# A mixture-of-experts layer on one core: the short chunk's down products stacked, shorter routing, four weight chunks split later

## The chip, the cores and the metric

The kernel runs on one core of a Trainium2 chip. The metric is the device time of one execution in microseconds (us), as a median over runs. A tile here has 128 partitions; T is 512 tokens.

## The reference, cut to what matters

Inputs: x of 8 groups x 1024 tokens x 256, float32. The first layer adds a gated linear scan (`q * scan(sigmoid(a), kv)` of three projections of a normalised x). The second layer adds a mixture of experts:

```python
logits = jnp.einsum('GSM,ME->GSE', x, router_w)          # 8 experts
dispatch, combine = _gating_top2(logits, C)              # C = 256 places per group and expert
expert_inputs = jnp.einsum('GSEC,GSM->EGCM', dispatch, x)
layer_w0 = jnp.einsum('EGCM,EMH->EGCH', expert_inputs, w0_kernel)   # H = 1368
layer_w1 = jnp.einsum('EGCM,EMH->EGCH', expert_inputs, w1_kernel)
hidden = jax.nn.gelu(layer_w0, approximate=True) * layer_w1
expert_outputs = jnp.einsum('EGCH,EHM->EGCM', hidden, wo_kernel)
out = jnp.einsum('EGCM,GSEC->GSM', expert_outputs, combine)
```

A token goes to its two best experts; a place number of 256 or more drops it. Every product is made in float32r with operands split into a high part (rounded) and a low part (the rest): high x high + high x low + low x high. The router's product is made in float32.

## The kernel before, in words

All order is written out by hand, engine by engine, with semaphores between them; nothing is a loop on the chip.

**Phase 1** has a step per group g (`step`). TensorE projects the group (`third`, line 1503: 12 blocks of 6 products with 512 columns), transposes (1519, 1532, 1544), and for the group before makes the router's logits (`route`, 1556: the 128 tokens of a tile are the stationary operand, the router's 8 columns stream; 4 tiles x 2 halves, each float32 product being two passes, so 16 loads and products per half group), and the running count of masks (`count`, 1563 and 1567). VectorE chooses the two experts of the group two back (`choose`, 16 instructions) and places its tokens (`place`, 12 instructions), between scans, residuals and statistics. ScalarE makes sigmoids, normalisations, the router's input `x2nT` (799) and the exponent (803). GpSimd scatters records (gates, token, source) to their slots (658) and gathers rows (677). Between these, ScalarE (813, 814) and VectorE (1211, 1223) split expert 0's weight chunks as they arrive: `first_chunks` says which chunks in which step.

**Phase 2** has 8 experts x 4 tiles of 512 rows. The hidden size 1368 goes in 11 chunks: 10 of 128, and the short chunk, number 8, with 88 = 64 + 24. Per chunk TensorE makes gate (1691) and value (1714; 1705 for the short chunk), 6 products of 512 columns each, and two chunks later the down products of chunk hc - 2, in four blocks j of 128 rows: high x (high | low) with 512 columns (1730) and low x high with 256 (1732). At the tile's end the down products of chunks 8, 9 and 10 stand in a row. The chain of a chunk: gelu on ScalarE (912; 906, 907 and a copy 910 for the short one), product on VectorE (1440; 1429, 1434, 1437 for the short one), high part on ScalarE (922), low part on VectorE (1443), down products. ScalarE's and VectorE's programs keep this order, so gelu of chunk hc + 1 stands behind the high part of chunk hc. In the fourth tile `next_weights(e, hc - 3)` follows on both engines from chunk 3 on (895, 896; 1211, 1418), and for the last three chunks in the next expert's first tile. Row blocks are scaled by the gates (956, 1410) and added to the output by GpSimd (726).

**The drain.** The first two tiles of expert 0 run beside the last groups' remaining steps (`drain(t, hc)`); there the down products use three products of 256 columns each (1725, 1727, 1732), as in the last tile of all. The last tile keeps the down products of chunks 5 to 10 to its end (`down_rows`). TensorE waits for all 11 of expert 0's splits before it begins tile 0.

## Time and profile before

| | us |
|---|---|
| median of 3 runs | 1645.25 |
| lowest, highest | 1642.83, 1646.39 |
| the profiled execution's own time | 1658.51 |
| its span | 1656.8 |
| TensorE, VectorE, ScalarE, GpSimd busy | 1620.5, 939.8, 762.3, 506.1 |

A row of a timeline has the start, the duration, the engine (PE TensorE products, PEld its weight loads, DVE VectorE, ACT ScalarE, POOL GpSimd), the line, the operation, the tiles written<-read, and in brackets how long the engine was idle before it and for whom. "x2" means that two like instructions are merged. The mean granted TensorE clock was 0.993 of full.

### The profile page before, as it was taken

The page shows a single profiled execution, that of the slowest core. Times are in us where ns is not written, and L with a number is a line of the kernel's source. Part 1 is how long each engine was busy: PE and PEld are TensorE (multiplying, and loading weights), DVE is VectorE, ACT ScalarE, POOL GpSimd, SP SyncE. Part 2 cuts the span into 40 slices and gives each one's busy share as a digit, 9 for nine tenths or more (in the row PEclk, how much of TensorE's full clock was granted, in tenths as well). Part 3 has the DMA queues.
Part 4 walks back from the last instruction along what each step waited for, and adds up shares of the span by engine and source line. Part 5 has one row for each costly group of instructions (what it writes and reads, how often), then busy time and mean ns, then how long its engine had stood idle before and what let it go on. Part 6 is the DMA issues. An engine that isn't in the chain of part 4 may idle for free.

```text
span 1656.8 us, 22948 instructions
## 1 busy us (share of the span) xinstructions
PE 1620.5 (98%) x8450; PEld 1396.0 (84%) x8450; DVE 939.8 (57%) x1955; ACT 762.3 (46%) x1389; POOL 506.1 (31%) x433
## 2 busy tenths in 40 slices
PE   7999899799999999999999999999999999999998
PEld 6888788688888888888888888888888888888887
DVE  7999754345644564447544654466445644475453
ACT  5777545234433453336333543345334533453333
POOL 2156566563222222222222222222222222222211
PEclk9999999899999999999999999999999999999999
DMA  7553121025422342225211522243223422351211
GB/s 169 160 160 122 53 80 45 13 41 120 86 38 37 81 93 37 39 43 124 39 36 36 135 38 39 39 109 71 39 39 82 93 36 38 64 109 33 36 13 13
DMA packets 193848, 110.94 MB, mean 67 GB/s; under 512 B 96008, under 2 KB 189640, under 8 KB 193736
## 3 DMA queue, kind: packets, MB, share of 16 engines
q1 hardware_dynamic: 165064, 75.37, 18.1%
q0 software_dynamic: 28672, 34.10, 12.8%
q8 instruction: 67, 1.10, 0.3%
q14 instruction: 45, 0.37, 0.1%
HBM read 60.11 MB, written 34.61 MB: 57 GB/s over the span
## 4 chain that ended last, share of the span: by engine, by line
PE 79%; DVE 6%; issue 4%; ACT 3%; SPq 3%; POOL 2%; DMA 2%; another core or an unknown queue 1%; POOLq 0%; ACTq 0%; DVEq 0%
PE bank L1691 23%; PE bank L1714 21%; PE bank L1730 14%; PE bank L1732 8%; PE bank L1503 7%; DVE y L1440 2%; PE bank L1556 1%; PE bank L1705 1%; SPq L509 1%; ACT hhi L922 1%; DVE hlo L1443 1%; SPq L426 1%; POOL slots L658 1%; POOL out L726 1%
## 5 line engine op out<-in xcount | busy, mean ns | idle before, releaser
L726 POOL DMA_INDIRECT out<-xring,slot_records x128 | 215.4, 1683 | 858.1 <-DVE xring L1410 792.9
L922 ACT ACTIVATE hhi<-y 128x512 fp32r<-128x512 f32 (+1 forms) x349 | 220.8, 633 | 508.7 <-DVE y L1440 427.6
L1730 PE MATMUL bank<-wo,hhi 128*128 128x512 f32 (+1 forms) x1276 | 443.7, 385 | 2.0 <-DVE hlo L1443 1.8
L1440 DVE TENSOR_TENSOR y<-bank,sig 128x512 f32<-128x512 f32 x320 | 220.9, 690 | 334.1 <-PE bank L1714 300.8
L1732 PE MATMUL bank<-wo,hlo 128*128 128x256 f32 x1396 | 382.2, 274 | 0.1
L1443 DVE TENSOR_TENSOR hlo<-y,hhi 128x512 fp32r<-128x512 f32 (+1 forms) x349 | 241.6, 692 | 243.9 <-ACT hhi L922 237.6
L912 ACT ACTIVATE sig<-bank 128x512 f32<-128x512 f32 x320 | 189.6, 593 | 209.2 <-PE bank L1691 181.9
L1730 PEld LDWEIGHTS bank<-wo,hhi 128*128 128x128 f32 (+1 forms) x1276 | 239.1, 187 | 50.5 <-DVE hlo L1443 4.0
L1732 PEld LDWEIGHTS bank<-wo,hlo 128*128 128x128 f32 x1396 | 261.6, 187 | 9.2 <-issue 0.8
L1691 PE MATMUL bank<-xThi,whi 128*128 128x512 f32 (+1 forms) x704 | 217.0, 389 | 7.4 <-issue 3.5
L1691 PE MATMUL bank<-xTlo,whi 128*128 128x512 f32 (+1 forms) x704 | 213.2, 383 | 0.0
L1691 PE MATMUL bank<-xThi,wlo 128*128 128x512 f32 (+1 forms) x704 | 212.7, 383 | 0.0
L1714 PE MATMUL bank<-xThi,whi 128*128 128x512 f32 x640 | 192.9, 381 | 1.2 <-DVE y L1440 0.8
L1714 PE MATMUL bank<-xTlo,whi 128*128 128x512 f32 x640 | 192.2, 380 | 0.0
L1714 PE MATMUL bank<-xThi,wlo 128*128 128x512 f32 x640 | 192.2, 380 | 0.0
L677 POOL DMA_INDIRECT rows<-x_rows,slot_records x128 | 129.4, 1011 | 122.0 <-DMA out<-xring,slot_records 88.6
L1691 PEld LDWEIGHTS bank<-xTlo,whi 128*128 128x128 f32 (+1 forms) x704 | 132.3, 188 | 27.0
L658 POOL DMA_INDIRECT slots<-records,sloti x128 | 128.3, 1002 | 82.5 <-DMA slots<-records,sloti 34.5
L1691 PEld LDWEIGHTS bank<-xThi,wlo 128*128 128x128 f32 (+1 forms) x704 | 132.4, 188 | 24.5
L1714 PEld LDWEIGHTS bank<-xThi,whi 128*128 128x128 f32 x640 | 120.1, 188 | 23.5 <-DVE y L1440 1.5
L1714 PEld LDWEIGHTS bank<-xTlo,whi 128*128 128x128 f32 x640 | 120.4, 188 | 20.8
L1714 PEld LDWEIGHTS bank<-xThi,wlo 128*128 128x128 f32 x640 | 120.1, 188 | 20.7
(147 smaller groups left out, 1730.6 us busy)
## 6 DMA issues: line engine op xcount, KB each, us to landing
stage<-in_L_ffn_w_kernel SPq DMA_DIRECT2D x160, 128.0 KB
rows<-rows SPq DMA_DIRECT2D x448, 32.0 KB, 1.9
stage<-in_L_ffn_wo_kernel SPq DMA_DIRECT2D x80, 128.0 KB
xring<-in_L_attn_x SPq DMA_DIRECT2D x16, 512.0 KB
out<-xring SPq DMA_DIRECT2D x16, 512.0 KB
x_rows<-rows SPq DMA_DIRECT2D x16, 512.0 KB
slots<-records,sloti POOLq DMA_INDIRECT x128
rows<-x_rows,slot_records POOLq DMA_INDIRECT x128
```

The costliest lines, as they stand in the source:

```text
L658: pool.indirect_dma_start(slots[:, :], bass.IndirectOffsetOnAxis(sloti[:, g.ring(RING), k, t:t + 1], 0), records[:, g.ring(RING), t, :], N ...
L677: pool.indirect_dma_start(rows2[:, p, j, :], None, x2_rows[t][:, :], bass.IndirectOffsetOnAxis(idx, 0)).then_inc(rows_loaded[p], 16)
L726: pool.indirect_dma_start(out_rows, bass.IndirectOffsetOnAxis(idx, 0), ysb[:, t % 2, j, :], None, compute_op=ALU.add).then_inc(added, 16)
L912: act.activation(gel[0:n, hc % 2, :], up_gate(e, t, hc)[0:n, :], ACT.Gelu_apprx_tanh).then_inc(gelu_done, 1)
L922: act.activation(h_high(e, t, hc)[0:n, :], hf[0:n, hc % 2, :], ACT.Copy).then_inc(h_hi, 1)
L1440: dve.tensor_tensor(hf[0:n, hc % 2, :], up_value(e, t, hc)[0:n, :], gel[0:n, hc % 2, :], ALU.mult).then_inc(mul_done, 1)
L1443: dve.tensor_tensor(h_low(e, t, hc)[0:n, :], hf[0:n, hc % 2, :], h_high(e, t, hc)[0:n, :].bitcast(F32), ALU.subtract).then_inc(h_lo, 1)
L1503: last = pe.matmul(lines(dst[:, :]), (wThi, wTlo)[wp][:, k, cols], lines((xThi, xTlo)[xp][:, h, k, :]), start=m == 0 and k == 0, stop=m == ...
L1691: last = pe.matmul(lines(up_gate(e, t, hc)[0:n, :]), (whi, wlo)[wp][:, hc, at:at + n], lines((xThi, xTlo)[xp][:, t % 2, k, :]), start=m == ...
L1714: last = pe.matmul(lines(up_value(e, t, hc)[:, :]), (whi, wlo)[wp][:, hc, at:at + P], lines((xThi, xTlo)[xp][:, t % 2, k, :]), start=m == ...
L1730: pe.matmul(lines(yb[j][:, :]), high, lines(wo[0:n, hc, :, :].rearrange("p s c -> p (s c)")), start=hc == 0, stop=end, skip_group_check=True)
L1732: return pe.matmul(lines(y_half(e, t, j)), low, lines(wo[0:n, hc, 0, :]), start=False, stop=end, skip_group_check=True)
```

## The change

Down products of the short chunk, outside the drain and the last tile (there the same operands are used, the rests without row groups). The high tile takes 120 rows: 64 high rows, 32 low rows (0 to 31) against the same weights, and the 24 rest rows, moved to partition 96. The low tile likewise: the 64 high rows against low weights, low rows 32 to 63, and the low parts of the rest. So two products of 256 columns per block carry all but one: rest high x rest low, 24 rows deep, whose operands are copied into four groups of 32 partitions (`h_rest`, `wo_rest`), one per block.

```diff
@@ -1716,8 +1743,28 @@
                                          start=m == 0 and k == 0, stop=m == 2 and k == KD - 1)
                 last.then_inc(up1, 1)
 
+            def down_rest(e, t, j):
+
+                if in_drain(e, t) or final(e, t):
+                    rest, high = slice(REST, REST + HR), h_high(e, t, SHORT)[REST:REST + HR, j * P:(j + 1) * P]
+                else:
+                    rest, high = slice(32 * j, 32 * j + HR), h_rest[32 * j:32 * j + HR, :]
+                return pe.matmul(lines(y_half(e, t, j)), high, lines(wo_rest[rest, :]), start=False, stop=False,
+                                 skip_group_check=True)
+
+            def down_short(e, t, j):
+
+                n = REST + HR
+                for h, part in ((h_high, 0), (h_low, 1)):
+                    last = pe.matmul(lines(y_half(e, t, j)), h(e, t, SHORT)[0:n, j * P:(j + 1) * P],
+                                     lines(wo[0:n, SHORT, part, :]), start=False, stop=False, skip_group_check=True)
+                return last
+
...
@@ -1744,6 +1791,13 @@
                 if (e, t, hc) == (0, 2, 0):
 
                     pe.wait_ge(cum_read, G)
+                if hc == SHORT and not (in_drain(e, t) or final(e, t)):
+                    for j in range(FJ):
+                        down_short(e, t, j)
+                    for j in range(FJ):
+                        last = down_rest(e, t, j)
+                    last.then_inc(down, 1)
+                    return
                 for j in range(FJ):
                     last = down_block(e, t, hc, j)
                     if hc == HC - 1 and j < FJ - 1:
```

ScalarE copies for it, and VectorE subtracts in three pieces; the weights are loaded and split to match:

```diff
+                        if hc == SHORT:
+                            for j in range(FJ):
+                                act.activation(h_rest[32 * j:32 * j + HR, :],
+                                               hf[REST:REST + HR, hc % 2, j * P:(j + 1) * P], ACT.Copy)
+                            act.activation(h_low(e, t, hc)[0:HF, :], hf[0:HF, hc % 2, :], ACT.Copy)
+                            n = REST + HR
                         act.activation(h_high(e, t, hc)[0:n, :], hf[0:n, hc % 2, :], ACT.Copy).then_inc(h_hi, 1)
...
-                        dve.tensor_tensor(h_low(e, t, hc)[0:n, :], hf[0:n, hc % 2, :], h_high(e, t, hc)[0:n, :].bitcast(F32),
-                                          ALU.subtract).then_inc(h_lo, 1)
+                        high, low = h_high(e, t, hc), h_low(e, t, hc)
+                        if hc == SHORT:
+                            for to, a, m in ((low[LOW:REST], 32, 32), (low[REST:REST + HR], REST, HR),
+                                             (high[LOW:REST], 0, 32)):
+                                split = dve.tensor_tensor(to, hf[a:a + m, hc % 2, :], high[a:a + m].bitcast(F32),
+                                                          ALU.subtract)
+                            split.then_inc(h_lo, 1)
+                        else:
+                            dve.tensor_tensor(low[0:n, :], hf[0:n, hc % 2, :], high[0:n, :].bitcast(F32),
+                                              ALU.subtract).then_inc(h_lo, 1)
...
                 act.activation(wq_part(wThi, n), wq_raw(n), ACT.Copy).then_inc(wq_hi, 1)
 
+            def high_out_weights(hc):
+
+                raw_out = stage[:, hc % STAGES, UCOL:WCOL]
+                if hc != SHORT:
+                    return act.activation(wo[:, hc, 0, :], raw_out, ACT.Copy)
+                n = REST + HR
+                act.activation(wo[0:n, hc, 0, :], raw_out[0:n, :], ACT.Copy)
+                act.activation(wo[LOW:REST, hc, 1, :], raw_out[32:HF, :], ACT.Copy)
...
+            def low_out_weights(hc):
+
+                raw_out, high = stage[:, hc % STAGES, UCOL:WCOL], wo[:, hc, 0, :].bitcast(F32)
+                if hc != SHORT:
+                    return dve.tensor_tensor(wo[:, hc, 1, :], raw_out, high, ALU.subtract)
+                rest = slice(REST, REST + HR)
+                for j in range(FJ):
+                    dve.tensor_tensor(wo_rest[32 * j:32 * j + HR, :], raw_out[rest, :], high[rest, :], ALU.subtract)
+                return dve.tensor_tensor(wo[0:HF, hc, 1, :], raw_out[0:HF, :], high[0:HF, :], ALU.subtract)
...
-            sync.dma_start(stage[0:n, s, 2 * KD * P:WCOL],
-                           wo_in[bass.ds(e, 1), c, :].rearrange("o h m -> h (o m)")).then_inc(w_staged[s], 16)
...
+            for to, a, m in ((0, 0, HF), (LOW, 0, 32), (REST, HF, HR)) if hc == SHORT else ((0, 0, n),):
+                sync.dma_start(stage[to:to + m, s, UCOL:WCOL],
+                               wo_in[bass.ds(e, 1), at + a:at + a + m, :].rearrange("o h m -> h (o m)")).then_inc(
+                                   w_staged[s], 16)
...
-            loads = [5 if c == SHORT else 3 for c in range(s, HC, STAGES)]
+            loads = [7 if c == SHORT else 3 for c in range(s, HC, STAGES)]
```

Gates: each of a token's two records now carries its own gate, so that VectorE's three instructions per tile (`gates`) go, and 956, 953 and 1410 take the gate from the record.

Routing: the router's 32 columns (8 and zeros) are the stationary operand and 128 tokens stream, to the four groups of 32 output partitions; ScalarE copies the logits (`copy_logits`), and TensorE transposes them back (`route_back`):

```diff
-                for j in range(HT):
-                    for k in range(KD):
-                        at = (h * HT + j) * E
-                        last = pe.matmul(lg[:, at:at + E], x2nT[:, k, j * P:(j + 1) * P], router[:, k, :],
-                                         start=k == 0, stop=k == KD - 1)
-                last.then_inc(logits, 1)
+                for k in range(KD):
+                    for j in range(HT):
+                        last = pe.matmul(lgT[j * QUAD:(j + 1) * QUAD, :], router[:, k, :],
+                                         x2nT[:, k, j * P:(j + 1) * P], start=k == 0, stop=k == KD - 1)
+                last.then_inc(logits_t, 1)
+
+            def route_back(g, h):
+                wait(pe, logits_copied, g, 2, h + 1)
+                at = h * HT * QUAD
+                pe.transpose(lg[:, at:at + LOGIT_ROWS], by_expert[0:LOGIT_ROWS, :],
+                             ident[0:LOGIT_ROWS, 0:LOGIT_ROWS]).then_inc(logits, 1)
 
...
 
-                    rest = TILES - t
-                    last = pe.matmul(cum[:, :, t + 1:TILES + 1, :], ones[:, :],
-                                     mask[:, :, t:t + 1, :].to_broadcast([P, 2, rest, E]),
+                    rest = TILES - t - 1
+                    if rest:
+                        pe.matmul(cum[:, :, t + 1:TILES, :], ones[:, :],
+                                  mask[:, :, t:t + 1, :].to_broadcast([P, 2, rest, E]), start=False, stop=False)
+                    last = pe.matmul(cum[:, 1, :, :], ones[:, :], mask[:, 0, t:t + 1, :].to_broadcast([P, TILES, E]),
                                      start=False, stop=t == TILES - 1)
                 last.then_inc(counted, 1)
...
+
+            def copy_logits(g, h):
+                wait(act, logits_t, g, 2, h + 1)
+                act.activation(by_expert, lgT, ACT.Copy).then_inc(logits_copied, 1)
```

`route_back` stands in phase 1 after `third(i, 0, 0, "q")` and after `transpose2(i.plus(-1), 1)`, `copy_logits` after the sigmoids; in the drain they stand in chunks 0 and 1 (group before the last), 10 and then 0 and 1 of tile 1 (last group). VectorE's `choose(..., 0, 2)` moves from chunk 0 to chunk 1 in both.

Placing has 6 instructions instead of 12; dropped tokens go to slots behind the others:

```diff
                 if n == 0:
                     wait(dve, counted, g, 1, 1)
-                    dve.tensor_scalar(cnt1[:, :], tot, float(CAP), None, ALU.min).then_inc(place_chain, 1)
+                    dve.tensor_tensor(pos[:, :, :, :], cum, mask[:, :, :, :], ALU.mult).then_inc(cum_read, 1)
                 elif n == 1:
-                    dve.tensor_tensor(pos[:, 0, :, :], cum[:, 0, 0:TILES, :], first_mask, ALU.mult)
...
+                elif n == 2:
+                    wait(dve, place_chain, g, 2, 1)
+                    dve.tensor_scalar(dropped[:, :, :], psel[:, :, :], float(CAP), float(NSLOT), ALU.is_ge, ALU.mult)
+                elif n == 3:
                     dve.scalar_tensor_tensor(out=slotf[:, :, :], in0=top[:, :, :], scalar=-float(ESLOTS),
                                              in1=psel[:, :, :], op0=ALU.mult, op1=ALU.add).then_inc(place_chain, 1)
...
+                elif n == 4:
+                    wait(dve, place_chain, g, 2, 2)
+                    dve.scalar_tensor_tensor(out=sloti[:, g.ring(RING)].rearrange("p k t -> p (k t)"),
                                              in0=slotf[:, :, :].rearrange("p k t -> p (k t)"),
-                                             scalar=float(E * ESLOTS + g.value * CAP), in1=dump[:, g.parity],
...
+                                             scalar=float(E * ESLOTS + g.value * CAP),
+                                             in1=dropped[:, :, :].rearrange("p k t -> p (k t)"),
+                                             op0=ALU.add, op1=ALU.add)
                 else:
-                    dve.tensor_scalar(row[:, :, TOK].bitcast(I32), tokid[:, :], float(g.value * S), None,
+                    dve.tensor_scalar(records[:, g.ring(RING), :, :, TOK].bitcast(I32),
+                                      tokid[:, :].unsqueeze(1).to_broadcast([P, 2, TILES]), float(g.value * S), None,
                                       ALU.add).then_inc(routed, 1)
 
```

Weights of expert 0: chunks 7 to 10 leave phase 1 (steps 4 to 7 on VectorE) for the drain, and TensorE waits chunk by chunk:

```diff
-        first_chunks = {-1: (0,), 0: (1, 2), 1: (3, 4), 2: (5, 6), 3: (7,), 4: (8,), 5: (9,), 6: (10,)}
...
+        first_chunks = {-1: (0,), 0: (1, 2), 1: (3, 4), 2: (5, 6)}
+        drain_chunks = {1: 7, 2: 8, 5: 9, 7: 10}
...
-                if (t, hc) == (0, 0):
+                if t == 0 and hc in drain_chunks:
+                    first_weights(drain_chunks[hc])
+                if (t, hc) == (0, 1):
                     choose(before_last, 0, 2)
...
 
-            pe.wait_ge(w_split0, HC)
-
             def up_chunk(e, t, hc):
 
                 c = HC * t + hc
-                if t == 0:
+                if (e, t) == (0, 0):
+                    pe.wait_ge(w_split0, hc + 1)
+                elif t == 0:
 
```

GpSimd also clears the router's tile at the start, and SyncE waits for that ahead of the router's load; SyncE's wait for all splits ahead of the experts stays.

## Rows read from the trace of the kernel before

**Rows 1.** The page, part 1: busy us (share of the span) xinstructions
```profile
PE 1620.5 (98%) x8450; PEld 1396.0 (84%) x8450; DVE 939.8 (57%) x1955; ACT 762.3 (46%) x1389; POOL 506.1 (31%) x433
```

**Rows 2.** Windows by stage: stretch, its us, busy (x) per engine, PEclk, DMA, GB/s
```profile
80.81:106.63 25.82, 25.50 (x162) 22.42 (x162) 24.66 (x87) 19.33 (x36) 15.56 (x15) 1.00 0.53 149
...
217.69:262.50 44.81, 43.09 (x264) 37.48 (x265) 24.41 (x67) 20.77 (x33) 29.69 (x29) 1.00 0.32 97
```

**Rows 3.** Timeline of TensorE in a phase 1 step: start us, us, what
```profile
150.73 0.43 PE L1567 MATMUL bank<-mask,ones 128*128 128x128 bf16 x8
...
152.45 1.85 PE L1556 MATMUL bank<-router,x2nT 128*128 128x8 f32 x16
154.15 0.69 PE L1503 MATMUL bank<-xThi,wThi 128*128 128x512 f32 x2
...
158.58 1.06 PE L1532 MATMUL bank<-ident,z 128*128 128x128 f32 x8 [0.63 <-ACT x2nT L799]
```

**Rows 4.** Timeline of TensorE at the end of an ordinary tile
```profile
682.36 0.39 PE L1730 MATMUL bank<-wo,hhi 88*128 88x512 f32 x1
682.59 0.27 PE L1732 MATMUL bank<-wo,hlo 88*128 88x256 f32 x1
682.70 0.39 PE L1730 MATMUL bank<-wo,hhi 88*128 88x512 f32 x1
...
683.73 0.39 PE L1730 MATMUL bank<-wo,hhi 128*128 128x512 f32 x1
...
685.08 0.38 PE L1730 MATMUL bank<-wo,hhi 128*128 128x512 f32 x1
```

**Rows 5.** Timeline of ScalarE and VectorE in the same tile
```profile
677.02 0.63 ACT L922 ACTIVATE hhi<-y 88x512 fp32r<-88x512 f32 x1 [1.57 <-DVE y L1437]
...
677.69 0.69 DVE L1443 TENSOR_TENSOR hlo<-y,hhi 88x512 fp32r<-88x512 f32 x1 [0.70 <-ACT hhi L922]
...
682.63 0.69 DVE L1440 TENSOR_TENSOR y<-bank,sig 128x512 f32<-128x512 f32 x1 [1.91 <-PE bank L1714]
...
684.02 0.69 DVE L1443 TENSOR_TENSOR hlo<-y,hhi 128x512 fp32r<-128x512 f32 x1 [0.70 <-ACT hhi L922]
```

**Rows 6.** Groups by line and form, ScalarE: busy us, mean ns, idle before
```profile
L895 ACT ACTIVATE whi<-stage 128x512 fp32r<-128x512 f32 x77 | 47.7, 619 | 15.6 <-DMA stage<-in_L_ffn_wo_kernel 15.5
...
L896 ACT ACTIVATE wo<-stage 128x256 fp32r<-128x256 f32 x77 | 31.0, 402 | 0.0
```

**Rows 7.** Timelines of an expert's fourth tile: ScalarE, VectorE, TensorE
```profile
939.89 0.63 ACT L922 ACTIVATE hhi<-y 88x512 fp32r<-88x512 f32 x1 [1.57 <-DVE y L1437]
940.70 0.64 ACT L895 ACTIVATE whi<-stage 128x512 fp32r<-128x512 f32 x1 [0.17 <-DMA stage<-in_L_ffn_wo_kernel]
941.24 0.40 ACT L896 ACTIVATE wo<-stage 128x256 fp32r<-128x256 f32 x1
...
941.67 0.69 DVE L1211 TENSOR_TENSOR wlo<-stage,whi 128x512 fp32r<-128x512 f32 x1 [0.42 <-ACT wo L896]
942.28 0.42 DVE L1418 TENSOR_TENSOR wo<-stage,wo 128x256 fp32r<-128x256 f32 x1
942.61 0.68 DVE L1440 TENSOR_TENSOR y<-bank,sig 128x512 f32<-128x512 f32 x1
...
945.77 0.68 DVE L1440 TENSOR_TENSOR y<-bank,sig 128x512 f32<-128x512 f32 x1
...
947.90 0.49 PE L1730 MATMUL bank<-wo,hhi 128*128 128x512 f32 x1 [0.16 <-DVE hlo L1443]
```

**Rows 8.** Timeline of TensorE in the last tile
```profile
1641.69 0.38 PE L1725 MATMUL bank<-wo,whi 128*128 128x256 f32 x1 [0.66 <-DVE hlo L1443]
```

**Rows 9.** Timeline of TensorE in tile 0 of expert 0
```profile
230.16 0.68 PE L1691 MATMUL bank<-xThi,whi 128*128 128x512 f32 x2 [0.17 <-ACT sig L912]
...
256.46 1.09 PE L1544 MATMUL bank<-ident,rows 128*128 128x128 f32 x8
```

**Rows 10.** Timeline of TensorE in tile 1 of expert 0
```profile
297.23 1.22 PE L1691 MATMUL bank<-xThi,whi 128*128 128x512 f32 x2 [2.54 <-issue]
```

More of the change, by code:

```diff
@@ L608, in _ @@
             pool.iota(fill[:, :, :, SRC].bitcast(I32), pattern=[[0, 2], [0, FJ]], base=2 * S, channel_multiplier=0)
-            for r in range(0, RING, 2):
-                pool.iota(records[:, r:r + 2, :, SRC].bitcast(I32), pattern=[[S, 2], [P, TILES]], base=0,
+            for r in range(RING):
+                pool.iota(records[:, r, :, :, SRC].bitcast(I32), pattern=[[0, 2], [P, TILES]], base=S * (r % 2),
                           channel_multiplier=1)
```

185 lines of the change are left out of this document (80 added, 105 removed).

## The prediction, made before the change was run

> **What bounds the kernel now.** The page's busy times come first: TensorE is busy for 1620.5 us of a span of 1656.8, VectorE for 939.8, ScalarE for 762.3 [rows 1]. The chain that ended last is TensorE for 79% of the span, so a microsecond taken off TensorE counts, and one added on another engine counts only where TensorE has to wait for it. The windows by stage say where that can be [rows 2]. In phase 1 a step takes 25.8 us with TensorE busy for 25.5 and VectorE for 24.7: two engines are full. The first drain tile (44.8 us) leaves VectorE 20 us of room. Inside a tile of the experts the timeline decides. TensorE runs without a gap, and three chunks of down products stand at the tile's end: the short chunk's from 682.36, chunk 9's from 683.73, chunk 10's from 685.08 [rows 4]. The last one needs a chain that runs ScalarE, VectorE, ScalarE, VectorE. For chunk 10 it starts at 682.63 and ends at 684.02 + 0.69 = 684.71, 0.37 us before it is needed [rows 5]. So at a tile's end the other engines are close behind. In the fourth tile of an expert, where the next expert's weights are split too, they are already behind: TensorE waits 0.16 us there for the low parts [rows 7].
>
> **Part 1, the stacked down products.** (a) TensorE. Four blocks take 683.73 - 682.36 = 1.37 us now, with 8 weight loads [rows 4]. After it there are 8 products of 256 columns at 0.11 us each (682.59 to 682.70) and 4 rests. The lower bound lets the rests run side by side: 9 x 0.11 = 1.0. The upper bound without other costs lets the loads go one behind another. Their price is in the router's row: 16 pairs whose products have 8 columns take 154.15 - 152.45 = 1.70 us, so a load of 128 columns costs 0.106 [rows 3]. Then 12 pairs take 1.33 and nothing is gained. I take 1.15, in the middle, since no row has row groups.
>
> (b) ScalarE and VectorE. ScalarE gets five copies ahead of the high part that VectorE waits for: four of 24x128 and one of 64x512. A copy with 512 columns takes 0.619, with 256 columns 0.402 [rows 6], which gives an estimate of 0.29 for 128, and copies follow one another 0.1 sooner than they last (540 ns between the two of 940.70 and 941.24, of which the first lasts 0.64) [rows 7]. So 4 x 0.19 + 0.52 = 1.28 us (bounds: 4 x 0 + 0.52 and 4 x 0.4 + 0.52). VectorE's one subtraction becomes three; each further one costs 0.61 (941.67 to 942.28) [rows 7]: 1.2 us.
>
> (c) Who waits, ordinary tile (22 of them). The short chunk's high part starts at 677.02 now, and at 678.3 then; its three low parts run from 678.97 to 680.9. Chunk 9's product on VectorE goes behind them, at 680.8, and so its high part at 681.5, chunk 10's gelu behind that at 682.05 to 682.65, chunk 10's product at 682.75 instead of 682.63, its low part ready at 684.85 instead of 684.71. TensorE wants it at 682.36 + 1.15 + 1.35 = 684.86. The product saving of 0.2 is thus just kept; bounds +0.3 and -0.2 per tile. I take -0.05, so -1 us in all.
>
> (d) The fourth tile (7 of them, experts 0 to 6). Here each chunk also carries a weight split on both engines, in the same order. VectorE's row is 0.42 idle for ScalarE's copy, then the split from 941.67, then at once chunk 9's product at 942.61 [rows 7]. Then: high part 939.89 + 1.28 = 941.17, low parts from 941.84, 3 x 0.61, split at 943.67, product at 944.6, which is 2.0 later. The next split waits for ScalarE's, which follows the late high part, so chunk 10's product moves from 945.77 to 947.76, also 2.0 later, and TensorE's last chunk from 947.90 to 949.9. Nothing gives this back in the tile. In some experts ScalarE waits for the staging DMA of that chunk, which swallows up to 0.7 of it: 1.8 on average, 12.6 us in all (bounds 7 x 1.2 and 7 x 2.5).
>
> (e) The last tile keeps chunks 5 to 10 to its end, and TensorE begins them at 1641.69 after 0.66 of waiting for chunk 9's low part [rows 8]. The same 1.28 + 1.2 stand ahead of that: +2.5 us.
>
> **Part 2, phase 1.** (a) Routing. It costs 1.70 each, 16 times [rows 3]. It will load 32 columns and stream 128, in two passes for each of 8 products. Bounds: 16 passes of 0.106 one by one, 1.7; 16 passes of 0.055 (half of the 256-column pitch) four at a time, 0.25. I take 1.0, passes at 0.106 of which neighbours in other column groups overlap in pairs. The transposition back adds 0.2, the running count gets seven more products per group; the 8 of now span 0.43 [rows 3], at most 0.054 each, less with the last one's length taken off: 0.24. So a step saves 2 x 0.7 - 2 x 0.2 - 0.24 = 0.8, and of the 0.63 that TensorE waits before the next step [rows 3] 0.2 is covered by the transposition: 1.0. VectorE must give the same. It loses six small instructions of placing; with 87 taking 24.66 us [rows 2] that is at most 6 x 0.28, and I take 0.6; from step 4 on it also loses a chunk's split, 0.94. So steps 2 to 7 gain 1.0 each and step 1 half: -6.5 us (bounds -11 and +3).
>
> (b) The drain. Four chunks' splits (0.93 on ScalarE, 0.94 on VectorE) move in. VectorE has room; ScalarE has none at two places. In chunk 1 of tile 0 the exponent now waits for VectorE's split and `choose` behind it; TensorE already waits 0.17 for that gelu at 230.16 [rows 9], so +1.15. In chunk 7 the split stands before the normalisation that TensorE's transposition waits for at 256.46 [rows 9]: +0.95. In tile 1 the choice starts a chunk's step later, behind the transposition back: +0.6. Three routings less give -1.5, transpositions and counts +0.6. Sum +1.8. SyncE's wait for all splits ends later, in chunk 7 of the drain; behind it stand only records and row moves of the third tile on, so nothing. The short chunk's two further loads cost SyncE 1.2 us of issue, with a chunk's time of slack. The gates taken from VectorE were hidden.
>
> **The sum.** -1 + 12.6 + 2.5 - 6.5 + 1.8 = +9.4 us. The profiled execution took 1658.5 (span 1656.8) and would take 1667.9; the median of the three runs is 1645.25, 13.3 lower, perhaps since waits such as the 2.54 us of [rows 10] are longer under the profiler. The sum goes on the median: 1654.6.
>
> **A rule weighed.** The router's rows put a full load at 0.106 us, one behind another. The Trainium skill (TensorE: Matmul & The Clock Gate, Part 3) says that products in different row or column groups overlap almost wholly; by it the rests would take the lower bound and routing 0.5 us, which is the first rival. The Trainium skill (TensorEngine Tiling (Array Packing), Key Properties) says that a change of tiling mode drains the engine; that is the second rival. No row of before shows either.
>
> **Rivals.** (A) The groups overlap fully and the chain costs less: routing at 0.45 takes 14 x 0.55 = 7.7 more off (two of the 16 lie where TensorE waits anyway), if VectorE follows; ordinary tiles give 0.2 each, -4.4 instead of -1; the small copies cost half, and the fourth tiles lose 1.2 instead of 1.8, 4 less. 1654.6 - 7.7 - 3.4 - 4 = 1639.5. It decides from the point where ScalarE's copies are under 0.1 each. For it: VectorE's relief in steps 4 to 7. Against it: the three subtractions of full length. 0.17 for faster. (B) The modes drain: 0.27 - 0.11 = 0.16 for each change, so 0.33 on each short chunk and each routing: 22 x 0.35 + 16 x 0.33 = 13 more, 1667.6; or TensorE's longer idle times (1.9 in fourth tiles, 3.1 in the last) drop its clock: after 2.54 idle a pair took 1.22 instead of the 0.6 of a pair at 2.4 GHz [rows 10], about 0.5 us for each of some five pairs. 0.2. (C) Both parts' gains and losses cancel, because the fourth tile's lag is partly hidden by late staging and routing gets near 0.5: 1646. 0.14. The forecast itself: 0.49.
>
> **Numbers.** A measurement of this kernel can tell 0.2%, 3.3 us. The range runs from rival A's end to rival B's, 1640 to 1669. Slower by more: 0.49 + 0.2 = 0.69; same 0.14; faster 0.17.
>
> **What would show it.** Fourth tiles: idle before the last chunk's first product of 1.5 to 2 us, ended by the low part. Last tile: a wait of 3 us instead of 0.66. Ordinary tiles: period unchanged within 0.2 us. Routing: the time from its first product to the next projection, 1.0 against 1.7. Drain: waits for gelu in chunk 3 and for the normalisation in chunk 8. If fourth tiles show under 1 us of wait, or steps of phase 1 fall below 24 us, the forecast is wrong.

## The result, and the profile after

The changed kernel takes 1684.5 us (median of 4 runs, 1683.1 to 1686.4), the kernel before 1645.0 on the same chip: a ratio of 1.0243, 95% interval 1.0230 to 1.0255. The direction was forecast, the size was not: +9.4 us were forecast and +39.5 came, outside the range.

The kernel before has medians of 1659 and 1661 us in two later sessions and of 1644 to 1646 in all others, so each ratio below is to the kernel before in the same session. A second profile of the kernel before has a span of 1642.9 us, 14 less than the one that the prediction rests on. The difference lies wholly ahead of the fourth tile's short chunk (409.2 against 395.2 us), so stages are compared below with the second profile. A tile's period is the time from the first gate product of one short chunk to that of the next.

| stretch, by the first product of the gate | before (second profile) | after | difference | forecast |
|---|---|---|---|---|
| up to the first tile | 210.5 | 204.1 | -6.3 | -6.5 |
| on to the fourth tile's short chunk | 184.7 | 193.2 | +8.5 | +1.8 |
| 20 ordinary tiles | 43.60 each | 44.38 each | +15.6 | -1 for 22 |
| 7 tile periods with the next expert's weights | 44.27 each | 46.46 each | +15.3 | +12.6 |
| the last two short chunks to the last product | 59.4 | 67.3 | +7.9 | +2.5 |

Executions differ most in the second row: last_tile_filled (below), which is the changed kernel up to its last tile, takes 190.7 us there, 6.0 more than before.

The page of the changed kernel, parts 1 and 4, against [rows 1]: TensorE's share falls, and 22% of the chain that ended last is VectorE's or ScalarE's.

```profile
PE 1623.0 (96%) x8638; PEld 1376.9 (82%) x8638; DVE 975.4 (58%) x1900; ACT 825.1 (49%) x1581; POOL 504.2 (30%) x433
...
PE 68%; DVE 13%; ACT 9%; issue 5%; POOL 3%; DMA 2%; SPq 0%; POOLq 0%; DVEq 0%; ACTq 0%
```

**Ordinary tile.** TensorE's timeline at a tile's end, against [rows 4]:

```profile
678.04 0.27 PE L1759 MATMUL bank<-wo,hhi 120*128 120x256 f32 x1
...
678.83 0.27 PE L1759 MATMUL bank<-wo,hlo 120*128 120x256 f32 x1
679.03 0.38 PE L1752 MATMUL bank<-wo_rest,h_rest 24*128 24x256 f32 x4
679.41 0.49 PE L1777 MATMUL bank<-wo,hhi 128*128 128x512 f32 x1
679.74 0.27 PE L1779 MATMUL bank<-wo,hlo 128*128 128x256 f32 x1
...
681.40 0.49 PE L1777 MATMUL bank<-wo,hhi 128*128 128x512 f32 x1 [0.37 <-DVE hlo L1462]
...
682.86 0.60 PE L1718 MATMUL bank<-xThi,whi 128*128 128x512 f32 x2
```

The four rests do run side by side (their starts are within 0.01 us). But they begin 0.20 after the last full product instead of 0.11, the next product comes 0.38 after them, and its own place is 0.33 long instead of 0.23. The short chunk takes 679.41 - 678.04 = 1.37 us, as much as before, and chunk 9's second product comes 0.10 late on top. Of the 0.38, only 0.31 are TensorE's own: the low part of chunk 9 ends at 678.66 + 0.69 = 679.35, 0.06 before that product, in this tile and in every ordinary tile behind it. Where nobody keeps TensorE waiting (four_groups_bare, below) the same place reads:

```profile
670.68 0.27 PE L1757 MATMUL bank<-wo,hlo 120*128 120x256 f32 x1
670.89 0.38 PE L1750 MATMUL bank<-wo_rest,h_rest 24*128 24x256 f32 x4
671.20 0.48 PE L1775 MATMUL bank<-wo,hhi 128*128 128x512 f32 x1
671.52 0.28 PE L1777 MATMUL bank<-wo,hlo 128*128 128x256 f32 x1
```

The next product comes 0.31 after the rests there, and the short chunk takes 1.31. In the changed kernel chunk 10 then waits 0.37 for its own low part. The timelines of ScalarE and VectorE say why, against [rows 5]:

```profile
672.70 1.26 ACT L953 ACTIVATE h_rest<-y 24x128 fp32r<-24x128 f32 x4 [1.57 <-DVE y L1448]
673.97 0.63 ACT L955 ACTIVATE hlo<-y 64x512 fp32r<-64x512 f32 x1
674.51 0.61 ACT L957 ACTIVATE hhi<-y 120x512 fp32r<-120x512 f32 x1
...
675.15 1.39 DVE L1458 TENSOR_TENSOR hlo<-y,hhi 32x512 fp32r<-32x512 f32 x2 [2.49 <-ACT hhi L957]
676.55 0.68 DVE L1458 TENSOR_TENSOR hhi<-y,hhi 32x512 fp32r<-32x512 f32 x1
677.27 0.69 DVE L1451 TENSOR_TENSOR y<-bank,sig 128x512 f32<-128x512 f32 x1
678.66 0.69 DVE L1462 TENSOR_TENSOR hlo<-y,hhi 128x512 fp32r<-128x512 f32 x1 [0.70 <-ACT hhi L957]
679.27 0.68 DVE L1451 TENSOR_TENSOR y<-bank,sig 128x512 f32<-128x512 f32 x1
680.66 0.69 DVE L1462 TENSOR_TENSOR hlo<-y,hhi 128x512 fp32r<-128x512 f32 x1 [0.70 <-ACT hhi L957]
```

The four copies follow one another at 0.32 us, not 0.19, and the high part ends 2.42 after their start instead of 0.63 (+1.79, forecast +1.28). VectorE needs 2.12 for three subtractions (forecast 1.83). Both together are 0.8 later than forecast.

**Fourth tile.** TensorE and VectorE in the tile of [rows 7]: both late chunks are waited for, 0.93 and 1.53 us.

```profile
945.55 0.69 DVE L1224 TENSOR_TENSOR wlo<-stage,whi 128x512 fp32r<-128x512 f32 x1
946.16 0.42 DVE L1215 TENSOR_TENSOR wo<-stage,wo 128x256 fp32r<-128x256 f32 x1
946.50 0.68 DVE L1451 TENSOR_TENSOR y<-bank,sig 128x512 f32<-128x512 f32 x1
...
949.65 0.68 DVE L1451 TENSOR_TENSOR y<-bank,sig 128x512 f32<-128x512 f32 x1
...
948.63 0.48 PE L1777 MATMUL bank<-wo,hhi 128*128 128x512 f32 x1 [0.93 <-DVE hlo L1462]
951.77 0.49 PE L1777 MATMUL bank<-wo,hhi 128*128 128x512 f32 x1 [1.53 <-DVE hlo L1462]
```

**Last tile.** TensorE, and the window behind the wait (columns as in [rows 2]):

```profile
1664.98 0.58 PE L1772 MATMUL bank<-wo,whi 128*128 128x256 f32 x1 [3.94 <-DVE hlo L1462]
1665.36 0.42 PE L1774 MATMUL bank<-wo,whi 128*128 128x256 f32 x1
```

```profile
1665.00:1670.20 5.20, 5.20 (x21) 4.75 (x22) 1.22 (x2) 0.63 (x1) 0.00 (x0) 0.50 0.00 0
```

The wait is 3.94 us instead of the 0.66 of [rows 8], and for the 5.2 us behind it the granted clock is 0.50, 1.2 GHz instead of 2.4: only 21 products. In this kernel's fourth tiles, after 1.53 us, it does not fall.

**Routing and drain**, TensorE and VectorE, and under them two windows (columns as in [rows 2]):

```profile
150.22 0.65 PE L1568 MATMUL bank<-x2nT,router 128*32 128x128 f32 x16
150.79 0.71 PE L1516 MATMUL bank<-xThi,wThi 128*128 128x512 f32 x2
...
216.72 0.68 PE L1718 MATMUL bank<-xThi,whi 128*128 128x512 f32 x2 [1.11 <-ACT sig L941]
223.93 1.94 PE L1545 MATMUL bank<-ident,z 128*128 128x128 f32 x8 [4.31 <-DVE xring L1067]
249.23 1.09 PE L1557 MATMUL bank<-ident,rows 128*128 128x128 f32 x8 [0.72 <-ACT rows L795]
...
257.61 0.29 PE L1581 MATMUL bank<-mask,before 128*128 128x128 bf16 x1 [3.24 <-DVE mask L1151]
...
220.32 1.72 DVE L1218 TENSOR_TENSOR wo_rest<-stage,wo 24x256 fp32r<-24x256 f32 x4
222.05 0.42 DVE L1219 TENSOR_TENSOR wo<-stage,wo 64x256 fp32r<-64x256 f32 x1
222.39 0.67 DVE L1067 TENSOR_TENSOR xring<-xring,bank 128x512 f32<-128x512 f32 x1
```

```profile
223.93:229.93 6.00, 6.00 (x24) 5.62 (x25) 2.93 (x9) 0.63 (x1) 4.15 (x5) 0.50 0.50 154
257.61:260.61 3.00, 3.00 (x26) 3.00 (x27) 1.50 (x4) 2.35 (x5) 2.39 (x3) 0.50 0.06 9
```

Routing takes 0.57 us instead of 1.70 [rows 3]. In the drain the two waits that were forecast are there (1.11, 0.72), and two that were not. One is 4.31 us for VectorE's residual, which stands behind the short chunk's own weight split with its five subtractions. The other is 3.24 us for the masks of the group before the last, whose last two steps on VectorE stand behind the short chunk's three subtractions in tile 0. Behind the two waits the granted clock is 0.50 for at least 6.0 and 3.0 us. The second wait is the stack's: it is 3.15 us with the stack alone, 1.88 and 1.16 in high_first and four_groups_bare (below), and under 0.3 with phase 1 alone.

### The profile page after: what moved, and what is told of

Same layout as the page of the kernel before. It is cut to its first block, busy times and chain, and to the rows that moved or that the text cites. A ratio compares the mean times of both kernels' runs of the same rounds, so it can differ in the third digit from the quotient of the medians.

```text
span 1683.7 us, 23469 instructions
## 1 busy us (share of the span) xinstructions
PE 1623.0 (96%) x8638; PEld 1376.9 (82%) x8638; DVE 975.4 (58%) x1900; ACT 825.1 (49%) x1581; POOL 504.2 (30%) x433
## 3 DMA queue, kind: packets, MB, share of 16 engines
q0 software_dynamic: 28672, 34.10, 12.6%
q8 instruction: 68, 1.11, 0.3%
## 4 chain that ended last, share of the span: by engine, by line
PE 68%; DVE 13%; ACT 9%; issue 5%; POOL 3%; DMA 2%; SPq 0%; POOLq 0%; DVEq 0%; ACTq 0%
PE bank L1718 23%; PE bank L1741 20%; PE bank L1777 12%; PE bank L1779 6%; ACT hhi L957 3%; PE bank L1516 3%; DVE y L1451 3%; POOL slots L663 2%; ACT h_rest L953 1%; DVE hlo L1462 1%; DVE hlo L1458 1%; DVE y L1448 1%; DVE y L1445 1%; DVE hhi L1458 1%; DVE y L1440 1%
## 5 line engine op out<-in xcount | busy, mean ns | idle before, releaser
L1777 PE MATMUL bank<-wo,hhi 128*128 128x512 f32 x1160 | 410.6, 389 | 22.6 <-DVE hlo L1462 22.6
L1779 PE MATMUL bank<-wo,hlo 128*128 128x256 f32 x1268 | 348.2, 275 | 0.0
L1462 DVE TENSOR_TENSOR hlo<-y,hhi 128x512 fp32r<-128x512 f32 x317 | 219.5, 692 | 221.2 <-ACT hhi L957 221.2
L1777 PEld LDWEIGHTS bank<-wo,hhi 128*128 128x128 f32 x1160 | 217.3, 187 | 76.7 <-DVE hlo L1462 36.1
L1779 PEld LDWEIGHTS bank<-wo,hlo 128*128 128x128 f32 x1268 | 238.7, 188 | 7.5
```

Source lines behind the costliest of these rows:

```text
L1462: dve.tensor_tensor(low[0:n, :], hf[0:n, hc % 2, :], high[0:n, :].bitcast(F32), ALU.subtract).then_inc(h_lo, 1)
L1777: pe.matmul(lines(yb[j][:, :]), high, lines(wo[0:n, hc, :, :].rearrange("p s c -> p (s c)")), start=hc == 0, stop=end, skip_group_check=True)
L1779: return pe.matmul(lines(y_half(e, t, j)), low, lines(wo[0:n, hc, 0, :]), start=False, stop=end, skip_group_check=True)
```

## The experiments

Theory 1: the stack loses in the tiles, since ScalarE's copies and VectorE's subtractions make the low parts late; phase 1 loses nothing. Rival 1: the changes of TensorE's tiling are what costs. Rival 2: phase 1 or the moved splits are the loser.

### The two parts, each alone

phase1_alone takes back every edit of the short chunk's down products; stack_alone has those edits only.

> Only the second part of the change: routing by expert, four chunks split in the drain; the short chunk's down products as before. Theory 1 (the whole loss sits in the tiles of the experts: from the fourth tile on the profiles differ by 31.1 us up to the last tile but one and by 7.6 us over the last two, 38.7 of the 39.5 measured): 1645 us, within 4 us of the kernel before, tile periods 43.59 again. Rival (phase 1 gives what the two profiles show, 8.0 us by the first short chunk and 3.8 more by the fourth tile): 1633 us, and then the stacked part alone must cost over 50.

> Only the first part: stacked down products of the short chunk with rests in four row groups; phase 1 as before. Theory 1: 1684 us, tile period 44.38 in ordinary tiles, a wait of 1.5 us before the last chunk's products in fourth tiles, a wait near 3.9 us in the last tile and half clock after it. Rival (phase 1 gives 12 us): 1695 us or more.

Phase 1 alone: 1642.8 us, ratio 0.9977 (0.9967 to 0.9987), faster than before, ordinary period 43.59. The stack alone: 1695.3, 1.0300 (1.0279 to 1.0321), period 44.37, and 23.3 us from the last short chunk to the last product. So the loss is the stack's, and the phase 1 rival (1633) is out. That holds for the drain too: from the first tile to the fourth tile's short chunk phase 1 alone takes 186.9 us, 2.2 more than before (1.8 forecast), and the rest of the +8.5 of the changed kernel comes with the stack. My 1684 for the stack was a miss: it takes 10.8 us more without the new phase 1 than with it by the medians, 9.4 by the ratios. 6.6 of that lie between the fourth tile and the last but one. There five periods with weights are 46.75 to 47.02, since TensorE waits 1.2 to 1.5 us before chunk 9 instead of 0.93; one is 48.03 and one 49.59, and in these two the granted clock falls. For the longer one:

```profile
956.38 0.48 PE L1788 MATMUL bank<-wo,hhi 128*128 128x512 f32 x1 [1.54 <-DVE hlo L1481]
```

```profile
957.00:963.60 6.60, 6.00 (x19) 4.63 (x18) 4.75 (x10) 3.35 (x7) 1.59 (x1) 0.50 0.45 105
```

### The rests' four products left out

```
-                        down_short(e, t, j)
-                    for j in range(FJ):
-                        last = down_rest(e, t, j)
+                        last = down_short(e, t, j)
```

> The changed kernel, but the four products of the rests are left out in all tiles but the drain's two and the last (the output lacks the rests' low parts there); ScalarE's and VectorE's work is untouched. Theory 1 (the chain of ScalarE and VectorE sets the tile's end): the wait for the low part before the last chunk grows from 0.37 to about 0.8 us and the period of ordinary tiles falls by under 0.15, to 44.3; 1681 us. Rival (TensorE's changes of row groups are what costs): period 43.6 or less, 1665 us.

Ratio 1.0256 (1.0233 to 1.0278), 1688.0 us, and the period stays at 44.37: no gain at all, and 7 us over the 1681 that I expected. TensorE only waits longer: in an ordinary tile 0.30 us for chunk 9 and 0.38 for chunk 10. In two fourth tiles, after waits of 1.86 us, the granted clock fell to 0.50; their periods are 47.7 and 47.8, the other five 46.4 to 46.7. The waits of TensorE between 700 and 1600 us (total us, times, longest), first of this kernel:

```profile
PE bank L1777 <- DVE hlo L1462: 22.6, 40, 1.9
```

then of the changed kernel:

```profile
PE bank L1777 <- DVE hlo L1462: 17.8, 25, 1.5
```

Rival 1 falls as the explanation of the ordinary tiles.

### The rests from one row group, without the four copies

```
-                if in_drain(e, t) or final(e, t):
+                if True:
...
-                            for j in range(FJ):
-                                act.activation(h_rest[32 * j:32 * j + HR, :],
-                                               hf[REST:REST + HR, hc % 2, j * P:(j + 1) * P], ACT.Copy)
```

> The changed kernel with the rests of all four blocks read from one row group, so without ScalarE's four copies of 24 rows. Theory 1: the chain is 1.26 us shorter, so ordinary tiles no longer wait for the low part; the four rests go one behind another, 3 x 0.11 more, so TensorE's short chunk takes 1.8 instead of 1.48 and the period is 43.9 to 44.1; fourth tiles lose 1.2 us less each, the last tile 1.2 less: 1665 to 1670 us. Rival (four row groups are what the stack needs): period over 44.6, 1690 us.

1667.2 us, 1.0129 (1.0109 to 1.0149), period 44.00: 19 us less than the changed kernel by the ratios, though its four rests are further apart. TensorE's timeline:

```profile
673.38 0.27 PE L1756 MATMUL bank<-wo,hlo 120*128 120x256 f32 x1
673.58 0.71 PE L1749 MATMUL bank<-wo_rest,hhi 24*128 24x256 f32 x4
674.23 0.49 PE L1774 MATMUL bank<-wo,hhi 128*128 128x512 f32 x1
```

From 673.58 to 674.23 it is 0.65 us, against 0.31 for four groups where TensorE doesn't wait. No ordinary tile waits for a low part now; the period's 0.41 above 43.59 is TensorE's own.

### ScalarE's order turned round

```
                         act.activation(h_high(e, t, hc)[0:n, :], hf[0:n, hc % 2, :], ACT.Copy).then_inc(h_hi, 1)
+                        if hc == SHORT:
+                            for j in range(FJ):
+                                copied = act.activation(h_rest[32 * j:32 * j + HR, :],
+                                                        hf[REST:REST + HR, hc % 2, j * P:(j + 1) * P], ACT.Copy)
+                            copied.then_inc(rest_copied, 1)
...
+                    pe.wait_ge(rest_copied, FT * e + t + 1)
                     for j in range(FJ):
                         last = down_rest(e, t, j)
```

> The changed kernel with ScalarE's order turned round: the high part first, then the four copies of the rests, with a semaphore of their own on which TensorE waits before the rests. The same work on every engine. Theory 1 (the delay of VectorE's three subtractions by 1.26 us is what makes ordinary tiles wait): ordinary period 43.7, fourth tiles up to 1.2 us shorter, last tile's wait 1.2 shorter: 1662 to 1668 us. Rival (ScalarE's amount of work counts, not its order): period 44.3 or more, 1680 us or more.

1657.4 us, 1.0076 (1.0056 to 1.0095), better than expected: period 43.64, periods with weights 45.3 to 45.6 instead of 46.46. The same work on every engine, in another order, is worth 27 of the 39.5 us. The waits between 700 and 1600 us:

```profile
PE bank L1780 <- DVE hlo L1465: 7.1, 5, 1.5
```

### The stack with the other engines as before

```
-                            for j in range(FJ):
+                            for j in range(FJ if (e, t) == (0, 0) else 0):
...
-                            act.activation(h_low(e, t, hc)[0:HF, :], hf[0:HF, hc % 2, :], ACT.Copy)
...
-                            for to, a, m in ((low[LOW:REST], 32, 32), (low[REST:REST + HR], REST, HR),
-                                             (high[LOW:REST], 0, 32)):
+                            for to, a, m in ((low[0:REST + HR], 0, REST + HR),):
```

> The changed kernel with its products on TensorE as they are, but the other engines at the short chunk as before: the copies of the rests are made in the first tile only, the copy of 64 rows is left out and one subtraction of 120 rows stands for the three (so the stacked operands hold other numbers than they should). Theory 1: TensorE's own part of the stack costs 0.11 us a tile (the timeline of the changed kernel has 1.37 for the short chunk as before, and 0.33 instead of 0.22 for the product behind it), so the ordinary period is 43.70; with phase 1 as in the changed kernel and some 1.2 us in the last tile for rests that alternate with other products: 1648 us. Rival (the stack saves TensorE 0.2 once nobody keeps it waiting): period 43.4, 1639 us.

1646.3 us, 1.0012 (1.0002 to 1.0021), period 43.64. So TensorE's own part costs 0.05 a tile and saves nothing even when nobody keeps it waiting: 1.31 us for the short chunk and 0.10 behind it, against 1.37. The 0.11 that I had read came from the 1.37 of the changed kernel, of which 0.06 is a wait. From the last short chunk to the end it is 18.5 us against 16.95 with phase 1 alone, 1.55 for rests that alternate with other products. This kernel is 3.5 thousandths (5.8 us) behind phase 1 alone, each by its own ratio; by the profiles 4.2 us of it lie ahead of the fourth tile's short chunk, and the 4.31 us of the drain are still there (4.32).

### The last tile's wait filled

```
+                pe.wait_ge(gelu_done, done + HC - 1)
+                for n in range(14):
+                    pe.matmul(lines(bank[2][:, :]), whi[:, 9, 0:P], lines(xThi[:, t % 2, 0, :]), start=True, stop=True)
                 pe.wait_ge(h_lo, done + HC - 1)
```

> The changed kernel with 14 products of 512 columns into a bank that nobody reads, in TensorE's wait of the last tile (3.94 us). Theory 1 (about 2.6 of the 6.9 us that the last tile loses is half clock after that wait: 24 products at 0.21 instead of 0.11): the products after the wait keep a pitch of 0.11 and the end comes 2.5 us sooner, 1682 us. Rival (something other than the idle time slows them, operands or modes): pitch 0.21 again and 1684.5 us.

TensorE's timeline of this kernel, and under it a window as above:

```profile
1658.96 3.38 PE L1813 MATMUL bank<-xThi,whi 128*128 128x512 f32 x14 [0.33 <-ACT sig L941]
1662.57 0.38 PE L1772 MATMUL bank<-wo,whi 128*128 128x256 f32 x1 [0.23 <-DVE hlo L1462]
1662.79 0.28 PE L1774 MATMUL bank<-wo,whi 128*128 128x256 f32 x1
1662.91 0.28 PE L1779 MATMUL bank<-wo,wlo 128*128 128x256 f32 x1
```

```profile
1662.57:1667.77 5.20, 5.20 (x38) 4.70 (x39) 1.23 (x2) 1.11 (x2) 0.92 (x1) 1.00 0.00 0
```

The same products come at a pitch of 0.11 and a clock of 1.00, 38 in 5.2 us instead of 21, and it takes 21.75 us instead of 24.12 from the last short chunk to the last product. The idle time, not the operands, had halved the clock. The time of the whole run does not show it: 1683.7 us, ratio 1.0242 (1.0225 to 1.0259), its runs from 1680.8 to 1687.6.

### The kernel before, once more

> The kernel before, unchanged, for a second profile. The first one has 13 us more than the median of the plain runs, and the kernel with phase 1 alone lies 17 us ahead of it at the short chunk of the fourth tile, though its runs are only 3.8 us shorter. Theory 1 (the first profile had a rare delay in phase 1 and the first drain tiles, 1.0, 2.5 and 3.1 us of waits near 285, 297 and 310 us among it): this profile reaches that point near 396 us instead of 409.2, all else the same. Rival (every profiled execution of this kernel is that long): 409 us again.

One execution, 1644.7 us, the fourth tile's short chunk at 395.2: as theory 1 has it. "Rare delay" was not the right name, since the last four profiles (two_chunks, phase1_again, two_chunks_again, after_two_chunks) show such waits too, near 300 us and without a releaser. What they are stays open.

### The parts of phase 1

routing_alone is phase1_alone with the table of before, chunks_alone the kernel before with the table of after and TensorE's wait for each chunk; two_chunks lies between:

```
-first_chunks = {-1: (0,), 0: (1, 2), 1: (3, 4), 2: (5, 6)}
-drain_chunks = {1: 7, 2: 8, 5: 9, 7: 10}
+first_chunks = {-1: (0,), 0: (1, 2), 1: (3, 4), 2: (5, 6), 3: (7,), 4: (8,)}
+drain_chunks = {5: 9, 7: 10}
```

> Phase 1 of the changed kernel with its routing, counting and placing, the short chunk's products as before, and chunks 7 to 10 split in phase 1 as before. With both parts of phase 1 the steps up to the first tile take 5.1 us less by the profiles (205.4 against 210.5) and the end comes 1.2 (profiles) to 3.5 us (runs) sooner. Theory 1 (VectorE is as full as TensorE there, so shorter routing gives only what VectorE's lost placing instructions give, and the moved splits give the rest): first tile near 208, time within 2 us of the kernel before. Rival (TensorE's routing, 0.57 instead of 1.70 us for each of 16, carries it alone): first tile at 205 or earlier, 1640 us.

> The kernel before with four chunks' weight splits moved into the first drain tile, nothing else. Theory 1: steps 4 to 7 lose 0.94 us of VectorE's work each, of which some 2.5 us reach the first tile (208), and the drain tile gives them back (a wait for gelu in chunk 1 to 3 and for the normalisation): 1644 to 1646 us, no difference. Rival (the moved splits are what makes the kernel with phase 1 alone faster): 1641 us.

Routing alone: 0.9989 (0.9975 to 1.0003), first tile at 207.0. Moved splits alone: 1.0025 (1.0012 to 1.0037), first tile at 209.4, 4 us slower. Together 0.9977. Neither rival holds, and my "no difference" for the splits was a miss. Whether the moved splits add anything to the shorter routing is not shown, since the intervals of 0.9989 and 0.9977 overlap.

> The kernel with phase 1 alone, but chunks 7 and 8 split in phase 1 as before and only 9 and 10 in the drain. Routing alone gave 0.9989 and reached the first tile at 207.0 us, both parts gave 0.9977 and 205.4, the moved splits alone 1.0025. Theory (a moved split pays while VectorE is what a step waits for, and costs where a drain chunk waits for ScalarE: TensorE waits 1.11 and 1.64 us near 218 and 222.5 us behind chunk 7's split with both parts): first tile at 206.2, those two waits gone, 1640 to 1642 us. Rival (all four belong in the drain, each gives its share): 1643.5 us, half way between the two.

1654.7 us against 1660.8, 0.9961 (0.9947 to 0.9975), first tile at 214.7. The wait for gelu is gone and the one near 222.5 us is 0.51, as the theory has it; the ratio can't be set beside 0.9977, so it was repeated beside phase 1 alone.

> Phase 1 alone once more, beside the next kernel on one chip: the kernel before took 1646 us beside the first and 1661 beside the second, so the two ratios (0.9977 and 0.9961) can't be compared. Expected 0.9975.

> Phase 1 with only chunks 9 and 10 moved. Theory (chunk 7's split in chunk 1 of the drain is in TensorE's way, in phase 1 it is not): 0.996, and better than phase 1 alone by 0.1 to 0.2%. Rival (the better ratio came from the slower chip): the same as phase 1 alone, 0.9975.

0.9964 (0.9952 to 0.9976) for all four moved, 0.9957 (0.9944 to 0.9970) for two: the intervals overlap, and which is better stays open. Both beat the kernel before and the changed kernel. The profiles also show a wait that takes up a part of phase 1's gain. TensorE's timeline in the drain, of the first profile of before:

```profile
243.76 0.66 PE L1591 MATMUL bank<-ident,rows 128*128 128x128 f32 x4 [1.00 <-DMA rows<-x_rows,slot_records]
```

and of phase 1 alone, second time:

```profile
241.46 0.48 PE L1573 MATMUL bank<-ident,rows 128*128 128x128 f32 x1 [4.61 <-DMA rows<-x_rows,slot_records]
```

The first tile begins 7.2 us sooner (210.5 against 217.7, where the second stretch of [rows 2] begins), but the rows that the second tile needs come only 2.3 sooner, and the fourth tile's short chunk 0.9 sooner. A part of the gain turns into a wait for gathered rows. How much can't be read from this pair, since the second profiled execution took 1660.9 us, 6.7 more than the median of its kernel. The first profile of phase 1 alone beside the second one of before has hardly any such wait (1.12 against 0.97), and of 5.1 us at the first tile 2.9 are left at the fourth tile's short chunk.

### The short chunk's split, and the gates

after_two_chunks is the changed kernel with the table of two_chunks; gates_put_back is the changed kernel with this on VectorE, at chunk 5:

```
+                        if hc == PREPARE[0] and not in_drain(e, t) and (t < FT - 1 or not last):
+                            for n in range(3):
+                                dve.tensor_tensor(st1[:, 0, n, 0:FJ], halves[:, 0, 0:FJ], halves[:, 1, 0:FJ], ALU.mult)
```

> The changed kernel with chunks 7 and 8 split in phase 1 as before, 9 and 10 in the drain. In the changed kernel the transposition back of chunk 1 of the drain waits 4.31 us, with phase 1 alone 1.64, with the stack alone 0.54. Theory (the stacked short chunk's longer weight split, five subtractions instead of one, is what stands ahead of that transposition when it lies in the drain): that wait falls under 1 us and the end comes 2 to 4 us sooner, ratio to before 1.022. Rival (the short chunk's longer split costs the same wherever it stands): ratio 1.024.

The 4.31 us fall to 0.53 as the theory says, but the ratio is 1.0244 (1.0229 to 1.0260), the rival's. The cause of that wait is shown, and its removal is worth nothing. The next wait, for the gathered rows, is 6.60 us there, which may be what takes up the gain; but it is 4.61 and 4.79 with phase 1 alone and two_chunks beside it, and the changed kernel has no profile of that session, so this is not shown.

> The changed kernel with three instructions of 4 columns added on VectorE at chunk 5 of each tile after the drain, in the place where the kernel before computes its gates. The stack alone takes 10.8 us more than the stack with phase 1, and 6.6 of it lie between the fourth and the last tiles (fourth tiles 46.95 instead of 46.45, one of them 49.6). Theory 1 (VectorE's 0.6 us of gates come on top of its late work in fourth tiles): fourth tiles near 46.9, ordinary ones unchanged, 1688 us. Rival (the difference is the transfers' doing, not the gates'): fourth tiles 46.45, 1684.5 us.

1685.9 us, 1.0247 (1.0226 to 1.0268), periods with weights 46.45 to 46.55, the first one 46.73. So three bare instructions are not what makes the stack alone slower. Of its 6.6 us, 4.7 lie in the two periods where the clock fell, the rest in the longer waits before chunk 9. Why VectorE is later there, by the gates' waits for the records and for one another or by something else, was not tried and stays open.

## Why the prediction was wrong

- **Right: where to look.** TensorE waits for low parts at the tile's end, fourth tiles show 1.53 us (1.5 to 2 forecast), the last tile 3.94 (3), and the drain's waits for gelu and normalisation are 1.11 and 0.72 (1.15 and 0.95 forecast).
- **Right by luck: phase 1's total**, 6.3 (6.5 forecast). It was to come from 1.0 us in each of steps 2 to 7. Between the transpositions of `z` (now line 1545) six steps in a row last 23.80, 23.78, 24.40, 26.34, 25.29 and 25.49 us, against 24.90, 25.43, 25.40, 25.39, 25.62 and 26.63 in the second profile of before. The first ones gain up to 1.65, the fourth loses 0.95, and two fall below the 24 us that the prediction named as a sign against it. The total also varies from run to run: seven other kernels with this phase 1 reach the first tile at 204.2 to 207.0.
- **(c) of part 1, the step that failed, some 17 of the 30 us missed.** The forecast put the last low part at 684.85 and the need at 684.86, a balance of 0.01 us, and priced the error at +0.3 at most. Two terms were mis-sized: (b)'s copies at 0.19 apart, measured 0.32 (an overlap taken from a copy of 512 columns to ones of 128), and subtractions at 0.61, measured 0.70. Together 0.8, so chunk 10 waits 0.37 and even chunk 9, which the forecast did not look at, 0.06, and the period is 44.38 instead of 43.59, 22 times. high_first and one_row_group, which each take ScalarE's copies out of this chain, end the ordinary wait. The upper bound of (b), 0.4 a copy, was in the text but was not carried into (c)'s bounds.
- **(a) of part 1.** 1.15 was forecast, 1.31 measured where nobody waits, plus 0.10 behind. The rests do overlap, as rival A said, and the entry and the exit take it all back, as rival B said: 0.09 ahead, 0.20 behind and 0.10 on the next product are 0.39, near B's price of 0.33 for both changes, which B put on top of the 1.15. What four_groups_bare leaves of it all is 0.05 a tile. The Trainium skill (TensorEngine Tiling (Array Packing), Key Properties) says that a change of tiling mode drains TensorE; the rows agree, with 0.20 instead of 0.11 ahead and 0.31 instead of 0.11 behind. A slip in this step changed nothing: 12 loads at its 0.106 are 1.27, not 1.33. The same rivals on routing: 0.57 us, nearly A's 0.45.
- **(d).** +1.8 a tile forecast, +2.2 measured, the same two terms again.
- **(e).** +2.5 forecast, +7.2: 3.3 of wait, 2.4 of half clock after it, 1.55 of alternating rests. The clock stood in rival B at 0.5 us for each of some five pairs; it held for at least 5.2 us.
- **Part 2, (b), +1.8 forecast, +8.5 measured** (+6.0 in last_tile_filled). The moved splits were costed at 0.93 and 0.94 us each, but the short chunk's own split has five subtractions on VectorE, 1.72 us for the four rests' alone, and the residual behind it was not looked at. The forecast had no term for it, and taking that wait away gained nothing (after_two_chunks). It also had no term for the stack itself in the drain, where the masks come 3.24 us late, nor for the half clock behind both waits. Phase 1 alone has +2.2 here, so what is missing comes with the stack. How it divides was not tried.
- **The reference of the sum.** The first profile was 13 us above the runs; "longer under the profiler" was a guess, and the second profile (1644.7 us) speaks against it. The sum of differences did not depend on it.

## What to carry to other kernels

Where an engine's operand is ready 0.01 us ahead of need, every term of the chain that makes it has to be bounded, not only TensorE's saving: an overrun counts once per tile, a surplus never. Before splitting an operand to save products, put the copies that only late products need behind the one that releases the next engine; here that order alone was worth 27 us. And moving work off a full engine is no gain by itself: the moved splits alone lose 0.25%, shorter routing alone gives 0.1% (not clear of nothing), and both together give 0.2 to 0.4%.

## What the runs showed of the hardware

- Four products of 24 rows in four row groups start within 0.01 us, and routing's 16 products in four column groups take 0.57 us. But each visit to the small groups costs about 0.09 ahead, 0.20 behind (0.31 instead of 0.11) and 0.10 on the next product. That last part is no price of the groups: behind a plain wait the next product's place is 0.34 long too (681.40 in the changed kernel).
- Small copies on ScalarE (24x128, 0.31 us each) do not overlap: 0.32 apart, while the copy of 512 columns behind them is followed after 0.54 of its 0.63. VectorE's three subtractions with 32 or 24 rows start 0.70 apart, full ones before a smaller one 0.61; the four of 24x256 start 0.43 apart and last 0.42. Rows saved nothing: 24x256 lasts as long as 128x256. In these rows an instruction that doesn't overlap the one ahead of it reads or writes from another first partition (0, 32, 64 or 96) than that one, and those that overlap share both; no run was made to test this. The Trainium skill (VectorE: DVE Perf Modes, The TRN2 errata) has a fixed cost per instruction on both engines; 0.31 us for 128 columns against 0.63 for 512 agrees.
- Behind waits of 3.94 and 4.31 us TensorE's granted clock was 0.50 for at least 5.2 and 6.0 us. Behind shorter ones both happened: it stayed at 1.00 in the changed kernel's fourth tiles (1.53 us) and fell to 0.50 in the stack alone (1.54 us, before 956.38) and with the rests' products left out (1.86 us, twice). So the length of the last wait alone does not decide it.
